# Adding the value bias on VectorE, one chain of scales per step, and the order of gate, key and score products

## What is computed

```python
x = _ln(x, ln1_w, ln1_b)
qk = _silu(x @ Wqk.T + bqk)              # 64 wide
v = _silu(x @ Wv.T + bv)                 # 512 wide
heads = qk[..., None, :] * gamma + beta  # quad_q, lin_q, quad_k, lin_k, each through _rope
attn = relu(quad_q @ quad_k.T / G + bias) ** 2       # inside groups of G = 64 rows
lin_out = lin_q @ (lin_k.T @ v / n)                  # over all 512 rows
gate = _silu(x @ Wg.T + bg)
out = (gate * (attn @ v + lin_out)) @ Wo.T + bo
x1 = _layernorm(x_in + _ln(out, ln2_w, ln2_b))
```

## Time and profile before

| | |
|---|---|
| median of 3 runs | 910.99 us |
| the profiled execution's own time | 911.82 us |
| its span, first to last instruction | 910.0 us |
| PE busy | 887.6 us (98%) |
| DVE busy | 684.2 us (75%) |
| ACT busy | 549.5 us (60%) |
| POOL busy | 268.4 us (29%) |
| PE weight loads | 794.4 us (87%) |

### The profile page before, as it was taken

How to read it: one execution, slowest core, us unless ns; L and a number is a source line. 1 busy time by engine, 2 the same in 40 slices (tenths; PEclk the granted TensorE clock), 3 DMA queues, 4 the chain that set the end, 5 groups by cost and what they waited for, 6 DMA issues and landing times.

```text
span 910.0 us, 17150 instructions
## 1 busy us (share of the span) xinstructions
PE 887.6 (98%) x5768; PEld 794.4 (87%) x5768; DVE 684.2 (75%) x1684; ACT 549.5 (60%) x1009; POOL 268.4 (29%) x189
## 2 busy tenths in 40 slices
PE   8999999999999989999999999999999999999995
PEld 7778888888878879899999999999999999999985
DVE  7789899889888699676576675757665589987475
ACT  5646656755646746556556455555645568887475
POOL 1000011001010237347545254553534445542000
PEclk9999999999999999999999999999999999999998
DMA  5232233241325424539575464856577558777723
GB/s 169 85 136 70 76 107 108 82 131 54 113 97 173 162 49 88 128 118 258 140 224 135 152 194 95 248 144 195 131 235 191 134 142 241 226 205 200 238 70 116
DMA packets 70132, 133.44 MB, mean 147 GB/s; under 512 B 14334, under 2 KB 55095, under 8 KB 62776
## 3 DMA queue, kind: packets, MB, share of 16 engines
q1 hardware_dynamic: 49864, 107.68, 35.5%
q0 software_dynamic: 16512, 21.32, 13.9%
q10 hardware_dynamic: 3696, 3.67, 1.2%
HBM read 98.13 MB, written 33.46 MB: 145 GB/s over the span
## 4 chain that ended last, share of the span: by engine, by line
PE 58%; DVE 4%; DMA 2%; issue 1%; ACT 1%; DVEq 0%; ACTq 0%; SPq 0%
PE bank L1796 25%; PE bank L1871 25%; PE bank L1816 3%; PE bank L1822 3%; DMA k_wstage<-wall 2%; PE bank L1856 1%; DVE s_hl L1709 1%; PE bank L1894 0%; ACT s_h L1391 0%; DVE s_y L1451 0%; DVE k_wpj1l L1606 0%; ACT s_hh L1395 0%; PE bank L1913 0%; DVE k_wpj1h L1605 0%; DVE s_xb L1454 0%
## 5 line engine op out<-in xcount | busy, mean ns | idle before, releaser
L1391 ACT ACTIVATE s_h<-bank,k_bfc 128x512 f32<-128x512 f32 (+1 forms) x216 | 134.5, 623 | 199.6 <-PE bank L1871 195.0
L1709 DVE TENSOR_TENSOR s_hl<-s_h,s_hh 128x512 fp32r<-128x512 f32 (+1 forms) x204 | 123.6, 606 | 134.6 <-ACT s_hh L1395 133.4
L1255 POOL DMA_INDIRECT residual_sums<-s_y,s_dest x64 | 108.4, 1694 | 183.6 <-DVE s_y L1639 163.9
L1395 ACT ACTIVATE s_hh<-s_h 128x512 fp32r<-128x512 f32 (+1 forms) x216 | 122.9, 569 | 9.1
L1871 PE MATMUL bank<-k_uh,s_wfc0h 128*128 128x512 f32 (+1 forms) x384 | 120.4, 361 | 0.1
L1796 PE MATMUL bank<-k_wpj1l,s_hh 128*128 128x256 f32 x384 | 108.9, 284 | 0.0
L1796 PE MATMUL bank<-k_wpj1h,s_hh 128*128 128x256 f32 x384 | 108.3, 282 | 0.0
L1796 PE MATMUL bank<-k_wpj1h,s_hl 128*128 128x256 f32 x384 | 108.2, 282 | 0.0
L1796 PE MATMUL bank<-s_wpj0l,s_hh 128*128 128x256 f32 x344 | 96.8, 281 | 0.8 <-DVE s_hl L1709 0.8
L1796 PE MATMUL bank<-s_wpj0h,s_hh 128*128 128x256 f32 x344 | 96.6, 281 | 0.0
L1796 PE MATMUL bank<-s_wpj0h,s_hl 128*128 128x256 f32 x344 | 96.5, 280 | 0.0
(11 more groups left out here) (358 smaller groups left out, 2241.3 us busy)
## 6 DMA issues: line engine op xcount, KB each, us to landing
k_wstage<-wall SPq DMA_DIRECT2D x42, 1024.0 KB, 5.6
s_acc<-wall SPq DMA_DIRECT2D x14, 1024.0 KB, 7.0
s_x_res<-x SPq DMA_DIRECT2D x8, 512.0 KB, 4.6
x_rows<-s_x SPq DMA_DIRECT2D x8, 512.0 KB, 3.4
residual_sums<-s_x SPq DMA_DIRECT2D x8, 512.0 KB, 4.2
x_parts<-s_x1h SPq DMA_DIRECT2D x8, 512.0 KB, 2.6
x_parts<-s_x1l SPq DMA_DIRECT2D x8, 512.0 KB, 3.6
k_uh<-x_parts SPq DMA_DIRECT2D x8, 512.0 KB, 5.2
```

What stands on the lines that cost most here:

```text
L1255: pool.indirect_dma_start(RES, bass.IndirectOffsetOnAxis(dest[:, at:at + 1].bitcast(U32), 0), y[:, t, :], None, bounds_check=N + S - 1, co ...
L1391: nc.scalar.activation(h[j % 2][:, cols], b[:, cols], ACT.Gelu_apprx_tanh, bias=bfc[w][:, j:j + 1]).then_inc(h_ev, 1)
L1395: nc.scalar.activation(hh[j % RING][:, cols], h[j % 2][:, cols], ACT.Copy).then_inc(hh_rd, 1)
L1709: tt(hl[j % RING][:, cols], h[j % 2][:, cols], hh[j % RING][:, cols].bitcast(F32), ALU.subtract).then_inc(hl_rd, 1)
```

## The change

- Bias of v: the products L816 and L835 go, and `bv2` with its preparation. The bias row is loaded into all partitions (`bv_all`, 256 KB for 66 KB). DVE adds it while it moves the bank to `v` (`values_biased`, a new semaphore `v_biased`), and ACT does its silu within `v` in SBUF. In step 0 two adds stand behind each pair of preparatory instructions of `offs`; in later steps the four follow the heads.
- Scales: in steps 1 to 7 one chain serves the next batch, the output and the sums (up to twelve numbers a row); it stands behind the statistics of the output product. The buffers for it grow from 2 x TT to 3 x TT columns. The centred output goes to `qkr`, which must first be read by the DMA of lq, and z is written when x1 has been made from the old one. `query_low` goes ahead of the output's statistics, the squared scores between centring and scaling.
- PE: `gate()`, `keys()`, `scores()` in every step. In steps 0 and 1 the attention products of all four parts of u come first and the linear ones behind them.
- ACT: behind the second gate silu come x1, the kT copy, and `xn`.
- SP: lq's DMA and the load of x_in go ahead of the two stores of x1.

```diff
@@ sync, step
-                if last:
-                    sp.wait_ge(x1_rd, c + 1)
-                    sp.dma_start(bidx(x1_view, c), x1[:, :, :]).then_inc(x1_st, 16)
-                    sp.dma_start(bidx(res_view, c), x1[:, :, :]).then_inc(x1_st, 16)
...
-                first = is_int(b) and b == 0
-                if first:
+                if main:
                     queries_moved()
                 if ahead:
...
+                if last:
+                    sp.wait_ge(x1_rd, c + 1)
+                    sp.dma_start(bidx(x1_view, c), x1[:, :, :]).then_inc(x1_st, 16)
+                    sp.dma_start(bidx(res_view, c), x1[:, :, :]).then_inc(x1_st, 16)
@@ scalar, step
-                    for t in range(TT):
-                        act.wait_ge(v_mm, 4 * b + t + 1)
-                        nc.scalar.activation(v[:, t, :], bank[t][:, :], ACT.Silu).then_inc(v_ev, 1)
...
+                if main:
+                    for t in range(TT):
+                        act.wait_ge(v_biased, 4 * b + t + 1)
+                        nc.scalar.activation(v[:, t, :], v[:, t, :], ACT.Silu).then_inc(v_ev, 1)
...
                         queries()
-                        keys()
                         for m in range(KE):
+                            if last and m == 2:
+                                sums_normed()
+                            if m == 2:
+                                keys()
+                            if ahead and m == 2:
+                                ahead_normed()
                             act.wait_ge(g_mm, 4 * b + m + 1)
@@ vector
+            def values_biased(b, t):
+                dve.wait_ge(v_mm, 4 * b + t + 1)
+                tt(v[:, t, :], bank[t][:, :], bv_all[:, :], ALU.add).then_inc(v_biased, 1)
...
+                if merged and ahead:
+                    ahead_stats()
...
+                if main and not at(0):
+                    need(dve, u_mm, 4 * b)
+                    for t in range(TT):
+                        values_biased(b, t)
...
                     tt(x_res[:, :, :], x_res[:, :, :], ln2[:, 1:2, :].to_broadcast([P, TT, D]), ALU.add).then_inc(res_rd, 1)
+                    if merged:
+                        query_low()
+                    stats(yo, OUT, lambda t: t % 2 or dve.wait_ge(o_mm, 2 * (b - 1) + t // 2 + 1))
+                    now = slice(0 if ahead else OUT, SUM + TT if merged and last else SUM)
...
+                    if merged:
+                        shifts(now.start, now.stop)
...
+                    if merged and last:
+                        dve.wait_ge(lq_rd, 16 * b + 16)
...
+                    if merged:
+                        scores_squared()
                     dve.wait_ge(o_ev, 4 * b)
                     dve.wait_ge(res_rd, b)
+                    if merged and last:
+                        dve.wait_ge(x1_rd, c + 1)
+                    for t in range(TT):
+                        last_i = stt(z[:, t, :], centred[:, t, :], rs[:, OUT + t:OUT + t + 1], x_res[:, t, :], ALU.mult, ALU.add)
@@ vector, ahead of step 0
                 link(stt(offs[:, k, :], rope[:, 1, :], vec[:, c + 1:c + 2], offs[:, k, :], ALU.mult, ALU.add))
+                values_biased(0, 2 * k)
+                values_biased(0, 2 * k + 1)
@@ tensor, step
-                        mm(bank[t][:, :], ones2[:, :], bv2[:, :], start=True, stop=False)
...
-                    for stage in (gate, keys_and_scores) if at(0) else (keys_and_scores, gate):
-                        stage()
+                    gate()
+                    keys()
+                    scores()
                     pe.wait_ge(kT_ev, b + 1)
...
+                    if not last:
+                        for m in range(KE):
+                            if m < 3:
+                                pe.wait_ge(g_ev, 4 * b + m + 2)
+                            for t in range(TT):
+                                cols = slice(t * P, (t + 1) * P)
+                                mm(bank[1 + m][:, cols], v[:, t, m * P:(m + 1) * P], att[:, t, :], start=t == 0, stop=False,
+                                   skip_group_check=True)
                     pe.wait_ge(kvl_rd, b + 1)
                     pe.wait_ge(lq_rd, 16 * b + 16)
+                    if not last:
+                        for m in range(KE):
+                            rows = slice(m * P, (m + 1) * P)
+                            mm(bank[1 + m][:, :], kvh[:, rows], lq[:, :], start=False, stop=False, skip_group_check=True)
+                            mm(bank[1 + m][:, :], kvl[:, rows], lq[:, :], start=False, stop=True, skip_group_check=True).then_inc(u_mm, 1)
```

More of the change, by code:

```diff
@@ L229, in attention @@
         x1h, x1l = pair("x1", [P, KD, T])
[L230 to L234, removed]
+        st = sb("st", [P, 3 * TT, 6])
+        mean = sb("mean", [P, 3 * TT])
+        var, rs, tmp = sb("var", [P, 3 * TT]), sb("rs", [P, 3 * TT]), sb("tmp", [P, 3 * TT])
+        half = sb("half", [P, 3 * TT], I32)
+        shift = sb("shift", [P, 3 * TT])
+        OUT, SUM = TT, 2 * TT
         raw = wstage[:, :, :].rearrange("p a n -> p (a n)")
@@ L313, in _ @@
             load(ld_w[1], (raw_v, a["wv"]))
-            load(ld_c0, (raw_bv, a["rows"][:, 0, :]), (raw_bo[:, :], a["rows"][:, 1, 0:D]), (ones_raw[:, :], a["ones"]))
+            load(ld_c0, (bv_all[:, :], a["rows"][0:1, 0, :].to_broadcast([P, E])), (raw_bo[:, :], a["rows"][:, 1, 0:D]), (ones_raw[:, :], a["ones"]))
             load(ld_c1, (rope[:, :, :], a["rope"]))
@@ L381, in _ @@
         def _(pool):
-            for tile in (bv2, bo2):
+            for tile in (bo2,):
                 nc.gpsimd.memset(tile[:, :].bitcast(F32), 0.0).then_inc(zeroed, 1)
@@ L588, in step, with ahead_stats @@
                 c = b - 2
+                merged = main and not at(0)
                 if last:
                     dve.wait_ge(res_used, c + 1)
[L591 to L607, removed]
+                    stats([z[:, t, :] for t in range(TT)], SUM)
+                def ahead_stats():
+                    dve.wait_ge(ld_x, 16 * (b + 1))
+                    stats([x_in[:, t, :] for t in range(TT)], 0)
+                if merged and ahead:
+                    ahead_stats()
+                if last and not main:
+                    need(dve, x1_rd, c)
+                    moments(nc, link, st[:, SUM:, :], mean[:, SUM:], var[:, SUM:], tmp[:, SUM:])
+                    if at(B + 1):
+                        beside(4)
+                    rsqrt(nc, link, rs[:, SUM:], half[:, SUM:], var[:, SUM:], tmp[:, SUM:])
+                    shifts(SUM, SUM + TT)
                 if at(B + 1):
@@ L629, in query_low, with scores_squared @@
                     tt(qkr[QK:P, 1, :], heads[QK:P, 0, :], lq[QK:P, :].bitcast(F32), ALU.subtract).then_inc(lql_rd, 1)
[L631 to L664 removed]
+                def scores_squared():
                     dve.wait_ge(sc_mm, b + 1)
@@ L676, in step @@
+                if at(B):
+                    beside(3)
+                if main:
+                    if at(0):
+                        dve.wait_ge(ld_c, 16 * CONSTS)
+                        scores_squared()
                     dve.wait_ge(kv_ev, b + 1)
@@ L861, in step, with keys @@
                             last_i.then_inc(o_mm, 1)
-                def keys_and_scores():
+                def keys():
                     need(pe, u_ml, 4 * b)
@@ L868, in keys_and_scores, with scores @@
                     last_i.then_inc(kT_mm, 1)
+                def scores():
                     pe.wait_ge(heads_rd, 2 * b + 2)
```

101 lines of the change are left out of this document (48 added, 53 removed).

## The result

The changed kernel takes 924.12 us (median of 6, 922.6 to 929.82), the kernel before in the same batch 911.88: ratio 1.0141 (95%: 1.0124 to 1.0158), 12.2 us slower. The forecast was 916.9 us, 5.9 over the kernel before, with a range of 909.5 to 920.5. The profiled execution took 923.75 us, 11.93 more than that of before. I go through the views in the order of the prediction.

A forecast was written before the change was run, and what follows sets the result against it. PE's dense row of products was taken as the bound, with DVE having no room. Late operands give +3.65 us by the end of step 2 and +2.2 in steps 3 to 7: +5.9, 916.9 us, range 909.5 to 920.5.

The forecast's parts named there:

- What bounds the kernel: From step 2 on, PE runs a row of products without a gap; DVE, busy 30.03 of 32.96 us, has no room.
- the steady step: Steps 3 to 7: the key-value product waits for kT, typically 0.59 us longer per step, +2.2 us together.
- The lengthening of POOL's 2.36 us by DVE: Steps 3 to 7, after the output product: DVE's running `query_low` lengthens POOL's instruction by 0.16 us.
- at the full granted clock: PE from step 2 on: busy for the whole window (33.07 and 32.96 us) at full clock.
- the forecast case: Whole kernel: late operands outweigh removed products, +5.9 us, 916.9 us, own range 913.5 to 919.5; chance 0.56.
- Steps 0 to 2: First three steps: adds and late u delay DVE, +3.65 us at the end of step 2, PE wait of some 4.
- the wait of 1.8 at the transposes: Step 0: `xn` is ready at 33.0 instead of 30.96, so PE waits 1.8 us.
- The 7.5 us of the removed products: PE, eight steps: four products fewer in each, 32 x 0.234 us, all on PE's path.
- rival 1: Merged chain is in time: PE saves 8.2 us plus 1.5 of waits, 901 to 904 us; chance 0.12.
- the 0.1 saved at the gate: Gate products no longer follow the half-height scores: 0.1 us saved in each of seven steps.
- Rival 2: POOL doesn't hold the new chain: steps 3 to 7 -0.1 each, step 2 +2.0, 912.4 us; chance 0.18.
- Rival 3: DVE becomes the bound in each step as adds and waits add up: +10 us or more, 921; chance 0.07.

The follow-up runs named there:

- the filled kernel: The changed kernel with 9, 15 and 4 idle products put into PE's wait ahead of the key-value product in steps 1, 2 and 3 to 7: 918.80 us.
- the kernel with step 0 as before: The changed kernel with ACT's silus first, u's old product order, POOL's instructions behind z's scaling, and step 0's bias as a product: 907.58 us.

## Why the prediction was half right

**What bounds the kernel, and the steady step: right.** The step as a row of products that stalls at the key-value product when kT is late came out to 0.01 us in its start (22.04) and to 0.1 in its length (33.65 for 33.55). The 0.01 is in part luck: x1 began 0.07 us later than forecast, and what follows it was 0.06 shorter. The chain that ends with POOL's instruction, x1 ahead of kT, and the wait for it are in the rows, and three variants took them away one at a time: the order on ACT (32.28), POOL's place (33.13), the adds (waits of 0.77 to 1.33 left). The lengthening of POOL's 2.36 us by DVE is there as well, 2.64; I had 0.16 for it and it was 0.28, of which DVE felt little.

**The step that failed: "at the full granted clock".** I read PEclk 1.00 in the earlier trace rows and priced each wait at its own length, with nothing for what PE does behind it. That number belonged to a row of products without a gap, and the change made gaps. At full clock the late operands cost 7.0 us (5.9 forecast); the products behind three of them at half clock cost another 5.5. No rival of mine had this mechanism, so neither the likeliest time nor the upper end of the range, 920.5, had room for it. The upper bound of the forecast case (+8) held for what it described. Of the miss of 7.2 us another 0.9 is the kernel before itself, 911.88 in this batch for 910.99. The Trainium skill ("TensorE: Matmul & The Clock Gate", "HAM oscillation — how this bites in real kernels") warns that gaps between runs of products make the clock fall and that the next run starts slow. The rows of steps 1, 2 and 4 agree that it happens; I had not weighed it. The page's example has waits of about 3 to 5 us, though, and here 2.47 and 1.57 were enough: the measurement decides.

The trace of before had a case of it as well, outside the attention. In the experts PE stands still for 3.86 us, and the window around it is the only one of those from 10 to 900 us that isn't at 1.00:

```profile
322.12 0.28 PE L1880 MATMUL bank<-s_both,s_trib 128*128 128x256 bf16 x1 [3.86 <-DVE s_both L1459]
...
300.00:330.00 30.00, 25.23 (x147) 21.98 (x147) 22.85 (x54) 14.87 (x25) 7.92 (x6) 0.94 0.32 92
```

It was the row from which a wait of 4 us in step 2 could have been given a price for the clock.

**Steps 0 to 2: right in sum, less so in parts.** +3.65 forecast, +4.5 at full clock. Step 2 is right (+2.87 for +2.90). In step 1 DVE began its statistics 0.5 us later than I had (45.80 for 45.3) and the wait ended at 62.58 for 61.85. In step 0 the wait of 1.8 at the transposes was 1.49. The key-value product started 0.23 later in the step than before (28.06 - 11.97 for 27.68 - 11.82), where I had 0.2. But the 32 attention products behind the transposes took 3.49 us (34.18 to 37.67) for my 3.24.

**The 7.5 us of the removed products: too large.** 32 x 0.234 counts steps 0 and 1, in which PE waits for kvl and gives little back (0.35 and 0.31). It didn't enter the likeliest time, since each step was reckoned from its own chain, but it is the term on which rival 1 (901 to 904) stood. A second term of it fell too, the 0.1 saved at the gate. Behind the half-height scores the key-value product is the one that starts badly: 3.73 us to the next product in the kernel with step 0 as before (123.51 to 127.24), where it was 3.43 (125.13 to 128.56) in the kernel before. A step with no wait is 32.28, not 32.0.

**Rival 2** (POOL doesn't hold the chain) fell by the changed kernel's own rows and by the variant that makes it true (the late POOL instruction, 21.50 for 22.04). **Rival 3** (DVE is the bound, 921 and more) gave the nearer time, but not the cause: DVE is busy 28.88 of 33.65 us in step 3, less than before (30.03), and step 3 is as long as forecast. What went beyond it was PE's clock.

**What stays open.** Which waits bring the clock down. Of eight waits of 2 us or more ahead of the key-value product, in all kernels, six were followed by products at half clock and two were not (2.08 in the kernel with the key copy first, 2.59 in the one with the late POOL instruction). Of nearly thirty between 1 and 2 us two were, one of them with the same 1.57 us that in the step before did nothing. Nor is it only this product: the wait of 1.10 for kvl in step 0 was followed by half clock in two kernels, and 1.11 in two others was not. That the gaps are the cause is shown by the filled kernel; what picks among them was not tried. The split of 7.0 and 5.5 us is that of one execution each, and the mean clocks of the six runs (0.985 to 0.990) suggest that they differ in how many such stretches they have; the medians (918.80 and 924.12) give 5.3.

## What to carry to other kernels

A wait put into a dense row of products can cost more than its length: ask what the granted clock does behind it, and give it a price even where the stretch shows full clock before the change. When several results hang on one merged chain, look at which of their consumers stands nearest to the bound engine and let only that one's operand bypass the chain: here moving a 0.6 us copy of the keys ahead of x1 gave 7.2 us (924.12 to 916.91), more than the 4.8 of all the removed products. Price a removed instruction by the steps in which its engine is bound, not by its count.

## What the hardware showed that I had not expected

- Half clock after short gaps: a gap of 1.33 us was once followed by a key-value product of 5.40 us instead of 3.70 (the kernel with the bias as products, step 3), and gaps of 2.1 to 3.8 mostly so (5.12 to 6.74).
- Adding 9, 15 and 4 useless products in steps 1, 2 and 3 to 7 made the kernel 5.3 us faster.
- DVE's tiny operation (two SBUF inputs) again ended with POOL's: 128.38 beside 128.34 in the changed kernel, 1.67 us long without the adds, 0.18 with POOL elsewhere. The Trainium skill ("SBUF — State Buffer", "Who interferes with whom") has this exclusion, and the trace agrees.
